# Local attention: VectorE's order inside a step, FFN statistics one step sooner, gated products behind the added rows

## What is computed

```python
x = x + attn_a(layernorm(x));  x = x + ffn(layernorm(x))      # ffn is two layers of local attention and FFN
x = x + attn_b(layernorm(x));  x = x + ffn(layernorm(x))      # the same block a second time
x = x + attn_a2(layernorm(x)); x = x + experts(layernorm(x))
x = x + attn_b2(layernorm(x)); x = x + experts(layernorm(x))

def _layer(x, wqkv, qs, ksc, wo, lg, lb, w1, b1, w2, b2):     # used twice in each ffn block
    q, k, v = split(shift_token(x) @ wqkv)                    # 8 heads of 64
    q, k = rotary_xpos(l2norm(q) * qs, l2norm(k) * ksc)
    x = x + local_attention(q, k, v) @ wo                     # window 64, this block and the one before
    h = shift_token(x)                                        # upper 64 columns come from the row before
    h = (h - mean(h)) / sqrt(var(h) + 1e-5) * lg + lb
    a, g = split(h @ w1 + b1)                                 # 341 columns each
    return x + (a * gelu(g)) @ w2 + b2
```

## Time and profile before

| | us |
|---|---|
| median of 3 runs | 1938.3 (1935.96 to 1942.25) |
| the profiled execution | 1945.41 |
| its span | 1943.6 |
| TensorE busy in the span | 1622.5 (83%) |
| VectorE busy | 1223.0 (63%) |
| ScalarE busy | 1069.2 (55%) |
| GpSimd busy | 906.4 (47%) |

### The profile page before, as it was taken

The page is one execution under the profiler, slowest core; times in us unless marked ns, Lnnn a source line. Parts: engine busy times, 40 slices in busy tenths (PEclk is TensorE's granted clock), DMA queues, the critical chain, the costliest instruction groups (busy, mean ns, idle before and its releaser), DMA issues.

```text
span 1943.6 us, 37984 instructions
## 1 busy us (share of the span) xinstructions
PE 1622.5 (83%) x13323; PEld 1160.9 (60%) x13323; DVE 1223.0 (63%) x3746; ACT 1069.2 (55%) x2751; POOL 906.4 (47%) x668
## 2 busy tenths in 40 slices
PE   5999997799999966889887789999976666958787
PEld 5999995566666633334544466666644544646565
DVE  3556554887777634555763788777736975636555
ACT  3655563788888724556542578888842113324332
POOL 1333333776666511323443777667613673422134
PEclk8999998999999986999876899999987987968979
DMA  5000000111111100000000111111100001210012
GB/s 206 1 1 1 1 2 6 26 33 31 28 26 29 26 3 1 1 1 1 2 1 1 24 27 32 26 33 26 32 7 0 1 1 38 23 27 1 22 23 23
DMA packets 41082, 38.64 MB, mean 20 GB/s; under 512 B 21944, under 2 KB 32192, under 8 KB 40512
## 3 DMA queue, kind: packets, MB, share of 16 engines
q1 hardware_dynamic: 35264, 32.02, 6.3%
q0 software_dynamic: 5632, 4.20, 1.8%
HBM read 13.14 MB, written 4.20 MB: 9 GB/s over the span
## 4 chain that ended last, share of the span: by engine, by line
PE 46%; DVE 15%; issue 12%; POOL 7%; ACT 4%; POOLq 0%; DMA 0%; DVEq 0%; ACTq 0%; SPq 0%; another core or an unknown queue 0%
PE ps L682 4%; PE ps L328 3%; PE ps L483 3%; PE ps L586 3%; PE ps L492 3%; PE ps L900 3%; PE ps L529 3%; PE ps L908 2%; PE ps L495 2%; PE ps L543 2%; PE ps L598 2%; PE ps L695 2%; PE ps L561 2%; PE ps L502 2%; DVE g_ss L1639 2%
## 5 line engine op out<-in xcount | busy, mean ns | idle before, releaser
L977 ACT ACTIVATE arena<-ps 128x512 f32<-128x512 f32 (+4 forms) x670 | 356.6, 588 | 284.2 <-PE ps L328 103.8
L1214 ACT ACTIVATE arena<-ps 128x320 f32<-128x320 f32 (+4 forms) x256 | 132.4, 561 | 137.4 <-PE ps L682 134.5
L1114 ACT ACTIVATE arena<-arena,g_small 128x128 f32<-128x128 f32 x512 | 198.7, 406 | 0.5
L2197 POOL TENSOR_TENSOR arena<-arena,consts 128x512 f32<-128x512 f32 (+1 forms) x64 | 93.2, 1456 | 196.1 <-ACT arena L1214 196.0
L1610 DVE CUSTOM_DVE_ANT_0 arena<-ps,consts,g_ss 128x128 f32<-128x128 f32 x512 | 145.6, 347 | 58.7 <-PE ps L483 58.7
L2218 POOL TENSOR_TENSOR arena<-arena 128x512 f32<-128x512 f32 x64 | 81.8, 1278 | 176.8 <-DVE arena L1618 176.8
L682 PE MATMUL ps<-arena 32*128 32x160 f32 (+4 forms) x1024 | 122.3, 468 | 20.9 <-ACT arena L1214 10.2
L328 PE MATMUL ps<-consts,arena 128*128 128x128 f32 x400 | 80.9, 340 | 68.7 <-POOL arena L2176 19.5
L1617 DVE TENSOR_TENSOR arena<-ps,tabs 128x512 f32<-128x512 f32 x128 | 87.7, 685 | 52.4 <-ACT arena L1083 44.9
L328 PEld LDWEIGHTS ps<-consts,arena 128*128 128x128 f32 x400 | 55.7, 172 | 106.1 <-POOL arena L2176 24.2
L682 PEld LDWEIGHTS ps<-arena 32*128 32x128 f32 x1024 | 61.9, 213 | 88.6 <-ACT arena L1214 54.2
(11 more groups left out here) (256 smaller groups left out, 4200.0 us busy)
## 6 DMA issues: line engine op xcount, KB each, us to landing
arena<-arena SPq DMA_DIRECT2D x112, 128.0 KB, 2.3
weights<-in_w SPq DMA_DIRECT2D x1, 5069.0 KB, 24.2
weights<-in_w SPq DMA_DIRECT2D x1, 2052.0 KB, 12.7
arena<-Y SPq DMA_DIRECT2D x64, 32.0 KB
arena<-Y SPq DMA_DIRECT2D x64, 31.8 KB
consts<-in_c SPq DMA_DIRECT2D x1, 1278.0 KB, 8.7
sorted_rows<-X SPq DMA_DIRECT2D x1, 1024.0 KB, 5.1
X<-sorted_rows SPq DMA_DIRECT2D x4, 256.0 KB, 3.6
```

The lines of the kernel that those rows point to most:

```text
L977: copy = lambda o, i: act.activation(o, i, ACT.Copy)
L1114: last = act.activation(g_p[:, n % 2, 4 * hf + i, :], g_sc[:, 4 * hf + i, :], ACT.Exp, scale=-1.0, bias=g_mn[:, h:h + 1], accum_out=g_rs[: ...
L1214: act.activation(b_p[:, U % 2, 2 * gp:2 * gp + 2, at:at + n], ps[:, b:b + 2, 0:n], ACT.Exp, scale=float(HD) ** -0.5).then_inc(s.b_exp, 1)
L2197: pool.tensor_tensor(v, v, m.unsqueeze(1).broadcast_to([P, NG, n]), ALU.mult)\
```

## The change

Only the order of instructions on VectorE is changed, and the place of one power on GpSimd. No instruction is added or removed, and TensorE, ScalarE and SyncE have the same rows as before.

```diff
-                    first, group = (t + 4) // 4, (t - 7) // 4
+                    first, group = (t + 4) // 4, (t - 6) // 4
...
-                    if at_step(t, 7):
-                        dve.wait_ge(gs.sh, 176 * (m0 + group + 1))
-                        norm_stats(1, g_h)
                     if live(t):
                         minima(t, 0)
                     if fresh:
                         norm_var(0)
-                    if at_step(t, 7):
-                        norm_var(1)
                     if live(t):
                         minima(t, 1)
+                    if at_step(t, 6):
+                        dve.wait_ge(gs.sh, 176 * (m0 + group + 1))
+                        norm_stats(1, g_h)
+                        norm_var(1)
...
-                    if live(t - 2) and at_step(t, 10):
-                        add_out(t - 2)
-                    if live(t + 2):
-                        sums(t + 2)
-                    if live(t - 2) and not at_step(t, 10) and not at_step(t, 12):
-                        add_out(t - 2)
                     if at_step(t, 7):
                         need(dve, gs.hnt, m0 + group)
                         norm_apply(1, g_hn, g_h, gs.h2)
+                    early = at_step(t, 10) or at_step(t, 11)
+                    if live(t - 2) and early:
+                        add_out(t - 2)
+                    for lag, half, c in FFN_STEPS:
+                        if half == 1 and at_step(t, lag):
+                            mid((t - lag) // 4, c)
+                    if live(t + 2):
+                        sums(t + 2)
+                    if live(t - 2) and not early and not at_step(t, 12):
+                        add_out(t - 2)
...
-                    for lag, half, c in FFN_STEPS:
-                        if half == 1 and at_step(t, lag):
-                            mid((t - lag) // 4, c)
...
-                    if at_step(t, 7):
+                    if at_step(t, 6):
                         root4(1)
```

More of the change, by code:

```diff
@@ L1699, in windows @@
                         add_down((t - 12) // 4)
-                    if live(t - 2) and at_step(t, 12) and not at_step(t, 10):
+                    if live(t - 2) and at_step(t, 12):
                         add_out(t - 2)
-                    for lag, half, c in FFN_STEPS:
-                        if half == 1 and at_step(t, lag):
-                            mid((t - lag) // 4, c)
                     if live(t - 1):
```

## The result

| | before | after |
|---|---|---|
| median, us | 1939.5 (1935.96 to 1942.25, 4 runs) | 1969.3 (1965.61 to 1978.4, 4 runs) |
| ratio | | 1.0162, 95% interval 1.0136 to 1.0188 |
| span of the profiled execution | 1943.6 | 1963.8 |

The changed kernel is **slower**, by 29.8 us between the medians. That is the sign of the prediction. The value is 5.3 us above the 1964 forecast, inside the range (1950 to 1977) and 1.3 above the narrower band of 1960 to 1968. The kernel before has one run more here than in its table above, so its median is 1939.5 and not 1938.3.

The account below looks back on a forecast made before the run. TensorE was taken to set the pace, busy 42.57 of 44.10 us. Per stage 6.1 (group 0) + 7.8 (five periods) - 1.0 (tail) = 12.9, two stages 25.8, on the median 1938.3 gives 1964; range 1950 to 1977.

Parts of the forecast that it names:

- the narrower band of 1960 to 1968: Whole kernel: the median in us around the forecast itself, given a chance of 45%.
- The landing: Group 3's last `shift`, issued at 529.46, lands at 532.4; the statistics' wait makes step 18's rotary products 2.4 late.
- The rivals that lived from an earlier landing: Statistics' wait: breakeven (1933 to 1944, 8%) if it ends at 530.5; faster (1929, 7%), deciding at a landing of 529.97.
- scores of step 19: TensorE, step 19: `scores` start at 538.06, 0.75 later than before.
- the new wait for k: TensorE, step 19: L518 has to wait until k is scaled at 542.1, 1.5 later than before.
- `project_v`: TensorE, step 18: it follows the late `add_out` and starts at 536.6 instead of 535.07.
- L1470: VectorE, step 19: this normalisation, now ahead of `add_out`, takes 2.0 beside GpSimd's pair additions, 1.0 as low end.
- the rival of both additions: Step 19: both GpSimd pair additions block L1470, 1972 to 1976; 23% together with a late landing.
- no contention: Step 19: L1470 finds gaps between GpSimd's instructions and takes 1.0, giving 1957; chance 17%.
- +1.55: Each of five periods: `scores` of step 20 start at 548.87 against 547.32, 1.55 later; 7.8 a stage.
- Group 0: Steps 6 and 7: rotary products 4.25 late, L1470 adds 2.0, less 0.1, so 6.1 a stage.
- The tail: Step 31 and the tail: statistics removed from VectorE's path win 1.0 a stage (0 to 1.5).

Follow-up runs that it names:

- The third kernel: The changed kernel with statistics taken of rows of X and the shift wait one step later, in front of L1470 (output not the reference's): 1938.2 us, ratio 0.9990.

## Why the prediction was right, and where its terms were off

**The landing: right.** I took 532.4 for an issue at 529.46, 2.95 from issue to the end of the wait; after shows 2.98. The idle time in front of L1451 is 3.25 in step 18, forecast 3.2, and 2.97 in step 6, forecast 3. The third kernel shows that this wait carries the loss. The rivals that lived from an earlier landing fall with it.

**scores of step 19 and the new wait for k: right.** `scores` of step 18 to those of step 19: 548.94 - 536.74 = 12.20, and 537.31 - 525.78 = 11.53 before (the row below is TensorE of before), 0.67 later, forecast 0.75. L518 waits for k and stands 16.29 behind the `scores` of step 18, before 540.60 - 525.78 = 14.82: 1.47 late in all, forecast 1.5. `project_v` stands 547.53 - 536.74 = 10.79 behind those `scores`, before 535.07 - 525.78 = 9.29: 1.50 later, forecast 1.5.

```profile
525.78 1.10 PE L483 MATMUL ps<-arena 64*64 64x128 f32 x32
```

**L1470: size right, effect too large.** It was taken at 2.0 and runs for 2.28. One pair addition held it and not both, so the rival of both additions fell (the second listed; the prediction calls it the third), and so did that of no contention. The step from there to TensorE was wrong: I let `norm_out` and the minima of step 19 start by the old distances and had the rotary products done at 545.1, counted on the time scale of before. In the trace of after `norm_out` started earlier than worked out, by about 0.5, and that swallowed the excess. The period without the clock's part is 45.28, **+1.23 instead of +1.55**.

**Group 0: the waits slightly too large, the clock missing.** 7.2 and 7.3 instead of 6.1. `project_v` of step 6 waited 4.64 (timeline of TensorE, after), and the `scores` behind it ran at the lower clock:

```profile
409.88 1.75 PE L502 MATMUL ps<-weights,arena 128*128 128x512 f32 x2 [4.64 <-DVE Y L1633]
411.56 1.99 PE L483 MATMUL ps<-arena 64*64 64x128 f32 x32
```

Their excess over the usual 1.13 and 1.10 is 0.62 and 0.89, and 0.77 and 0.85 in the second stage, so the lower clock cost about 1.6 in each. The waits alone thus cost about 5.7 a stage, 0.4 less than forecast: the rotary products of step 6 were 4.1 late (forecast 4.25), and step 7 added 1.6 (forecast 1.9).

**The tail:** -0.2 and -1.7 against -1.0 each, -1.9 against -2.0 together.

**What was missing: the clock.** The sum added waits to a TensorE of constant speed. The new idle times of 1.4 to 4.6 us are followed, in some places and not in all, by a stretch mostly at 1.2 GHz, which costs 1.1 to 1.6 each time. In the ledger that is 3.2 in group 0, 1.3 in steps 8 to 10 of the second stage (behind a wait of 2.44; the 2.45 of the first stage was not followed by a fall) and 2.5 in steps 10 to 30 of the first (1.38 + 1.10), together some 7. The overlarge period had added 10 x 0.32 = 3.2 too much, and the waits of group 0 some 0.8. So the errors had opposite signs, and the sum came closer than its terms by luck.

**Terms that do not add.** Alone, on the kernel before, the statistics cost 39, L1470 32 and the gated products with the added rows 5; together they cost 31. A piece that is late in an in-order queue hides the next one's delay. Walking all parts along one timeline, as the prediction did, takes this into account.

## What to carry to other kernels

Before an instruction with a wait is moved forward in an in-order queue, take the latest landing (issue plus what the same queue's rows show) and compare it with the start of the instructions that will stand behind it; here it was 2.4 us late by the prediction's working, and issuing that DMA ahead of `lookback` brought the kernel back to the time before. Moving reads of a shared queue forward only passes the wait on unless the engine has idle time there: look for the gap first and put into it what fits. When a change gives TensorE new idle time, add a term for the clock behind it, and cost the first and last rounds of a loop apart from the steady ones.

## What the runs showed that was not expected

- **The clock falls after short idle times in a busy stretch.** 1.95 us of idle at L502 were followed by a stretch at a granted clock of 0.56. The same 1.43 was not followed by one in step 18 and was in step 22. In the kernel with the statistics alone, 1.85 and then 1.75 were followed by it:

```profile
506.40:509.90 3.50, 3.50 (x28) 1.60 (x21) 2.26 (x16) 0.60 (x1) 2.39 (x2) 0.62 0.07 17
```

  What decides in a single case stays open. That with useless matmuls in the gap it stayed at 1.00 is shown in the trace above.
- **Identical work, different length.** Steps 0 to 6 of the stages took 60.4 to 65.1 us in kernels that have the same order there. A single trace's stretch ahead of the change is thus no measure for the change, while a steady period without a fall of the clock mostly repeats within 0.03 us (44.04 to 44.06 in before).
- **Contention between VectorE and GpSimd shows as a step.** L1470's single parts of 128x128 have a median of 342 ns and a longest of 1431 ns in after (line L1470): most go through untouched, and beside the pair additions one of four is held for about one addition.
